# State loop and side-by-side experts: the skip term added on VectorE, expert pairs packed into one matmul output, and a new order of loads and gathers

## What is computed

```
# layer 0, state-space block, 8 heads of 64, per row tile
y   = Y_diag + Y_off            # (C B^T * decay mask) @ x  +  (C @ state) * exp(cumsum)
y   = y + x * D                 # the skip term
u   = u + (y * silu(z)) @ w_out     # times a gate from the adaLN vector
# layer 0, experts: 64 experts, top 8 of a softmax, at most 64 rows each
h2  = layer_norm(u) * scale + shift
sel = top_k(softmax(h2 @ gate_w.T), 8)
out[e] = (silu(rows[e] @ wg[e]) * (rows[e] @ wu[e])) @ wd[e]     # inner width 96
u   = u + gate * sum over the 8 of weight * out[expert, slot]
# layer 1: attention in a window of 64, 16 heads of 128; then an MLP of 2048 whose weights
# are 4-bit codes with scales: W = LUT[code] * scale
```

## Time and profile before

| | us |
|---|---|
| median of 3 runs | 800.57 |
| lowest and highest | 797.09, 804.24 |
| span of the profiled execution | 801.1 |

### The profile page before, as it was taken

The page is one execution under the profiler, slowest core; times in us unless marked ns, Lnnn a source line. Parts: engine busy times, 40 slices in busy tenths (PEclk is TensorE's granted clock), DMA queues, the critical chain, the costliest instruction groups (busy, mean ns, idle before and its releaser), DMA issues.

```text
span 801.1 us, 9617 instructions
## 1 busy us (share of the span) xinstructions
PE 620.3 (77%) x3248; PEld 469.8 (59%) x3248; DVE 508.0 (63%) x1121; ACT 283.7 (35%) x887; POOL 249.7 (31%) x288
## 2 busy tenths in 40 slices
PE   2997988740109789975385898898988789998996
PEld 0544766530008677763163665666666668887885
DVE  5547567833997536724677789889757636655444
ACT  2644544400103222332255665646646431111110
POOL 1228003275650000137545255251101126640000
PEclk9999999965559956987577999999999999999999
DMA  8900001049017996863112043150000000000000
GB/s 317 351 1 0 1 2 47 34 147 299 3 42 205 278 281 222 244 195 98 45 48 49 5 54 37 17 53 1 0 1 1 1 0 1 1 1 27 1 1 27
DMA packets 29808, 62.83 MB, mean 78 GB/s; under 512 B 5827, under 2 KB 13297, under 8 KB 29184
## 3 DMA queue, kind: packets, MB, share of 16 engines
q1 hardware_dynamic: 22336, 45.42, 18.1%
q0 software_dynamic: 7424, 16.80, 9.3%
HBM read 48.56 MB, written 17.83 MB: 83 GB/s over the span
## 4 chain that ended last, share of the span: by engine, by line
PE 53%; DVE 21%; issue 8%; ACT 8%; DMA 6%; POOL 2%; another core or an unknown queue 1%; SPq 1%; POOLq 0%; DVEq 0%; ACTq 0%
PE bank L1104 47%; DMA arena<-expert_in 4%; DVE arena L1054 2%; POOL expert_in L396 2%; ACT arena L594 2%; DVE arena L1013 2%; PE bank L1326 2%; PE bank L1444 1%; DVE arena L968 1%; DMA expert_out<-arena 1%; PE bank L1272 1%; ACT arena L612 1%; DMA arena<-in_wmod 1%; DVE arena L1002 1%
## 5 line engine op out<-in xcount | busy, mean ns | idle before, releaser
L1104 PE MATMUL bank<-arena 128*96 128x64 f32 (+9 forms) x2040 | 425.2, 367 | 64.0 <-issue 26.0
L1104 PEld LDWEIGHTS bank<-arena 128*128 128x128 f32 (+4 forms) x2040 | 295.3, 192 | 160.6 <-issue 100.9
L396 POOL DMA_INDIRECT expert_in<-arena x64 | 65.2, 1019 | 88.7 <-DVE arena L857 70.1
L410 POOL DMA_INDIRECT arena<-expert_out,arena x64 | 72.6, 1134 | 19.0 <-issue 18.5
L692 ACT ACTIVATE arena<-bank 128x512 f32<-128x512 f32 x32 | 19.1, 598 | 112.4 <-PE bank L1104 112.4
L1085 DVE TENSOR_TENSOR arena<-arena,bank 128x512 f32<-128x512 f32 x32 | 22.0, 687 | 56.1 <-ACT arena L692 56.1
L594 ACT ACTIVATE arena<-bank,arena 128x128 f32<-128x128 f32 x128 | 45.2, 383 | 25.2 <-DVE arena L1006 25.2
L1104 PE MATMUL bank<-h_hi,gu_hi 128*128 128x512 f32 x128 | 50.8, 397 | 0.5 <-ACT arena L695 0.5
L1104 PE MATMUL bank<-h_low,gu_hi 128*128 128x512 f32 x128 | 50.5, 394 | 0.0
L1104 PE MATMUL bank<-h_hi,low 128*128 128x512 f32 x128 | 50.1, 391 | 0.0
L434 POOL TENSOR_TENSOR low<-arena,gu_hi 128x128 fp32r<-128x128 f32 x64 | 29.7, 495 | 60.4 <-DVE dn_hi L1017 60.4
(11 more groups left out here) (200 smaller groups left out, 1024.2 us busy)
## 6 DMA issues: line engine op xcount, KB each, us to landing
arena<-in_wgu SPq DMA_DIRECT2D x32, 384.0 KB, 6.5
arena<-in_wd SPq DMA_DIRECT2D x32, 192.0 KB, 8.9
expert_in<-arena SPq DMA_DIRECT2D x1, 4096.0 KB, 23.9
arena<-expert_in SPq DMA_DIRECT2D x16, 256.0 KB, 7.2
expert_out<-arena POOLq DMA_DIRECT2D x16, 256.0 KB, 6.5
arena<-in_w SPq DMA_DIRECT2D x1, 2048.0 KB, 9.3
arena<-in_wmod SPq DMA_DIRECT2D x1, 1536.0 KB, 15.0
arena<-in_w_in SPq DMA_DIRECT2D x1, 1288.0 KB, 8.8
```

Source lines behind the costliest of these rows:

```text
L396: pool.indirect_dma_start(xin, bass.IndirectOffsetOnAxis(scatter8[:, t, k:k + 1], 0), h[:, t, :], None, bounds_check=SLOTS - 1, oob_is_err ...
L410: pool.indirect_dma_start(gath[t % 2][:, k, :], None, yex, bass.IndirectOffsetOnAxis(gather8[:, t, k:k + 1], 0), bounds_check=SLOTS - 1, o ...
L1104: return pe.matmul(o, lhsT, rhs, start=start, stop=stop, **kw)
```

## The change

Five things change in one diff.

1. **State loop.** It has two iterations fewer (`T + 2`). The skip term `xD[s]` is added on DVE to `yo_s`, and the sum to bank 3; the identity product goes. `w_out` is multiplied once by the gate (POOL), so the residual is one addition. The norm only subtracts and divides; scale and shift of h2 are applied by ACT as it copies transposed rows (`h2_cols`), both for the logits and in the experts. Softmax sums are left to one pass after the loop. Tiles are chosen and placed one by one, at s = t + 2. PE's order is new: transposes of h2 first, diagonal products late.
2. **Loads.** Nothing of the expert weights is loaded in the front; 12 pairs go out one after the other during the loop, one pair and one chunk of codes after it. Rows of `expert_in` are loaded on POOL's queue.
3. **Experts.** The rows are now stationary and the weights move (192 columns), two experts side by side in the two halves of the output's partitions. The product of gate and up is transposed (`hidden_T`, two a group) and copied by ACT. Results are copied out in one instruction, with three buffers.
4. **Decoding** takes 4 instructions instead of 7 for each half chunk.
5. **Gathers.** Tiles 0 and 1 ahead of the attention loop, then tile t + 2 after the rotary product of tile t.

Semaphores are merged and renamed too (`rowsT_mm`, `rowsT_ready`, `var_ready` and others). The diff, cut to its core:

```diff
-            for q in range(4):
+            for q, tile, early in ((0, 1, True), (1, 2, True), (2, 2, True), (3, 3, True), (6, 3, True), (12, 4, True), (4, 1, False),
+                                   (5, 2, False), (7, 4, False), (8, 5, False), (9, 6, False), (10, 7, False)):
+                sp.wait_ge(st_mm if early else yT_mm, tile)
                 load_pair(q)
             sp.wait_ge(yT_mm, T)
-            load_codes(0)
-            load_codes(1)
-            for q in range(4, NS):
-                load_pair(q)
-            for n in range(2, NEARLY):
+            load_pair(11)
+            for n in range(NEARLY):
                 load_codes(n)
...
+            def load_rows(g):
+                if g >= NX:
+                    pool.wait_ge(xgT_mm, g - NX + 1)
+                pool.dma_start(xg[g % NX], xin[4 * CAP * g:4 * CAP * (g + 1), :].rearrange("(q p) c -> p q c", p=P))\
+                    .then_inc(xg_loaded[g % NX], 16)
...
             for g in range(NG):
-                pool.wait_ge(ob_ready, 2 * (g + 1))
-                pool.dma_start(yex[4 * CAP * g:4 * CAP * (g + 1), :].rearrange("(e s) c -> s e c", s=CAP), ob[g % 2])
+                if g + NX < NG:
+                    load_rows(g + NX)
+                pool.wait_ge(ob_ready, g + 1)
+                pool.dma_start(yex[4 * CAP * g:4 * CAP * (g + 1), :].rearrange("(q p) c -> p q c", p=P), ob[g % 3])
...
-            for t in range(3):
-                gather(t)
+            gather(0)
+            gather(1)
...
-                if t + 3 < T:
-                    gather(t + 3)
+                if t + 2 < T:
+                    gather(t + 2)
...
--            for s in range(T + 4):
+            for s in range(T + 2):
+                if 0 <= s - 2:
+                    less_maximum(s - 2)
                 if s < T - 1:
                     state_after(s)
+                if 0 <= s - 2:
+                    choose(s - 2)
                 if s + 1 < T:
                     make_M(s + 1)
                 if 0 <= s - 1 < T:
...
-                    link(dve.tensor_tensor(h[:, t, :], bank[7][:, 0:DM], mod[0][:, 2, :], ALU.mult))
-                    dve.tensor_tensor(x[:, t, :], x[:, t, :], h[:, t, :], ALU.add).then_inc(x1_ready, 1)
+                    dve.tensor_tensor(x[:, t, :], x[:, t, :], bank[7][:, 0:DM], ALU.add).then_inc(x1_ready, 1)
...
+                if s < T:
+                    skip, y = xD[s], un_y[:, s % 2, :]
+                    if s >= 1:
+                        dve.wait_ge(yo_ready, s)
+                        link(dve.tensor_tensor(skip, skip, yo_s, ALU.add))
+                    dve.wait_ge(Yd_mm, s + 1)
+                    link(dve.tensor_tensor(y, skip, bank[3][:, :], ALU.add))
+                    dve.tensor_tensor(zs[:, s, :], zs[:, s, :], y, ALU.mult).then_inc(y_ready, 1)
...
-                    link(normed(h[:, t, :], x[:, t, :], t, mv[2], rstd[2]))
-                    link(dve.tensor_tensor(h[:, t, :], h[:, t, :], mod[0][:, 4, :], ALU.mult))
-                    dve.tensor_tensor(h[:, t, :], h[:, t, :], mod[0][:, 3, :], ALU.add).then_inc(h2_ready, 1)
+                    normed(h[:, t, :], x[:, t, :], t, mv[2], rstd[2]).then_inc(h2_ready, 1)
+                if 0 <= s - 2:
+                    place_rows(s - 2)
...
-                    mm(bank[3][:, :], ident, xD[s], start=True, stop=False, skip_group_check=True)
...
             def gate_up(g):
...
-                for e in range(4):
-                    for a in range(2):
-                        for j in range(KC):
-                            ins = mm(bank[2 + g % 2][0:FI, (4 * a + e) * CAP:(4 * a + e + 1) * CAP], w[:, a, j, :],
-                                     xgT[g % 2][:, 2 * (e // 2) + j, (e % 2) * CAP:(e % 2 + 1) * CAP], start=j == 0, stop=j == KC - 1)
+                for i in range(2):
+                    for j in range(KC):
+                        for e in range(2):
+                            ins = mm(bank[2 + g % 2][64 * e:64 * e + CAP, 2 * FI * i:2 * FI * (i + 1)],
+                                     xgT[g % 2][:, 2 * i + j, 64 * e:64 * e + CAP], w[:, :, j, :], start=j == 0, stop=j == KC - 1)
+            def hidden_T(g):
+                for i in range(2):
+                    ins = pe.transpose(bank[4 + g % 2][0:FI, i * P:(i + 1) * P], hid[g % 2][:, i, :], ident)
```

More of the change, by code:

```diff
@@ L90, in adaln_two_layers @@
         scatter8 = at(small + 432, T, TOPK).bitcast(u32)
+        h2_cols = at(small + 498, 2 * KC)
         wbc = at(small + 496, 1)
@@ L152, in adaln_two_layers @@
         PAIR = 4 * KC * FI + 2 * DM
-        slot_at = [X0 + PAIR * i if i < 4 else A0 + PAIR * (i - 4) for i in range(NS)]
+        slot_at = [X0 + PAIR * (i + 1) if i < 3 else A0 + PAIR * (i - 3) if i < 6 else X0 if i == 6 else A0 + PAIR * (i - 4) for i in range(NS)]
         wgu_s = [at(o, 2, 2 * KC * FI) for o in slot_at]
@@ L393, in _ @@
             for t in range(T):
-                pool.wait_ge(slots_ready, 1 + sum(t > last for last in LAST))
+                pool.wait_ge(slots_ready, t + 1)
                 for k in range(TOPK):
@@ L1298, in down @@
+            def down(g):
+                pe.wait_ge(hidT_ready, g + 1)
+                if g >= 2:
+                    pe.wait_ge(ob_ready, g - 1)
+                for i in range(2):
+                    for e in range(2):
+                        ins = mm(bank[6 + g % 2][64 * e:64 * e + CAP, i * DM:(i + 1) * DM],
+                                 hidT[g % 2][:, i * P + 64 * e:i * P + 64 * e + CAP], wd_s[(2 * g + i) % NS][:, e, :])
                 ins.then_inc(down_mm, 1)
-            pe.wait_ge(slots_ready, len(BATCHES))
+            pe.wait_ge(place_read, T)
@@ L1304, in _ @@
                     rows_T(g + 1)
+                if g >= 1:
+                    hidden_T(g - 1)
                 gate_up(g)
```

420 lines of the change are left out of this document (193 added, 227 removed).

## The result

The changed kernel takes 831.0 us (median of 4 executions, 829.67 to 832.97); the kernel before, timed beside it, 802.4. The medians differ by 29 us. The ratio is 1.038, 95% interval [1.032, 1.044]: slower. (It leaves out the slow one of the four executions of the kernel before, 811.64.) The prediction was 790, faster by 1%. Its direction was wrong, and 831 lies outside its range.

The account below looks back on a forecast made before the run. Bounds: POOL's scatters end the state loop, which PE paces; DMA and PE alternate in the experts; DVE is attention's busiest chain. 801.1 - 33.5 - 8 - 4 + 35 = 790.6, median 0.5 below: 790 us, range 774 to 812.

Parts of the forecast that it names:

- Both gaps of POOL: State loop: POOL idle 13.0 and 8.1 us between scatters, the second blamed on loads; closing only these gives -21 us.
- the burst: Loads from 172 to 200 us, nine pairs and two chunks, 6.4 MB at 275 GB/s; predicted to be gone.
- the loop's start, which does not move: State loop: its start stays, so tile 0 has slots at about 108 us instead of 130.
- The round, 12.1 to 12.2 us: State loop: a chain of 8.0 us on PE and 4.1 on DVE makes 12.1 us, 0.7 longer than before.
- slots late: Rival, state loop: PE's 2 us wait for h2 lowers its clock, six rounds 1.5 us longer; 797 us, chance 0.13.
- The headline edit: State loop: identity product leaves PE (0.87 us a round), DVE gets one addition (0.69 us); by itself no gain.
- the diagonal products lie beside it: State loop: the diagonal products are off the round's chain of 12.1 us across PE and DVE.
- the chain of 4.1 us on DVE: State loop: residual, moments, skip, y, product with z and norm, with handovers, before PE can transpose the next h2.
- hide under PE's 5.1: Experts: decoding on DVE and the product, at most 4.5 us a group, hide under PE's 5.1 us.
- The limit of 270 GB/s: Experts: DMA is the bound, 23.8 MB at 270 GB/s take 88 us up to the start of the last group.
- it has those 6.5 us to spare: Attention: PE idles 8 us more each time and returns at half clock, but has 6.5 us spare at the end.
- The bound of +45 for attention: Attention: upper bound of the +35 us cost, with the half clock on the chain.

Follow-up runs that it names:

- the run with PE kept busy: The changed kernel with six unread products of 256 columns added at the end of each state-loop iteration, filling PE's wait for h2: ratio to before 1.032.
- the kernel before with the late gathers: The kernel before with one edit: gathers of two tiles ahead of the attention loop, then those of tile t + 2, as in the changed kernel: ratio 1.076.
- The edits of the codes' order: Two separate edits of the changed kernel: two chunks decoded ahead, ratio to before 1.038; codes from the third chunk on issued on POOL's queue, ratio 1.029.
- the kernel with the lost rows spread: The changed kernel, with zero-weight assignments that found no room reading scattered rows of expert_out instead of all reading its last row: ratio to before 1.030.
- with the gathers ahead: The changed kernel with only the gather order put back: three tiles ahead of the attention loop, then those of tile t + 3: ratio to before 0.969.

## Why the prediction was wrong, step by step

**State loop and scatter, -33.5 predicted, -23.5 measured.** Both gaps of POOL and the burst ended, as predicted; the cause given for the second gap, the full DMA, is not borne out. Tile 4's first scatter was put at 108 + 4 x 12.2 = 156.8 and came at 167.4. Two terms make up the 10.6:
- Slots of tile 0 at 108; they came at 112.8 and the scatter at 113.9, 5.9 later. The step that failed is "the loop's start, which does not move": it moved by 4.0. POOL's new product was put at nothing because POOL had time; the DVE instruction beside it took 2.38 us, and PE behind that waited and had the half clock for longer. The other 1.9 are the working of the first iterations and the start of the scatter.
- The round, 12.1 to 12.2 us, was 13.44: 1.2 each over four rounds. This is the rival "slots late". The prediction gave it 0.13 because no row showed a gap of 2 us in the loop; the run with PE kept busy shows its size, 1.7 us on PE's part of the round (9.8 for 8.1), of which DVE's part, 3.6 for 4.1, gave 0.5 back.

From there POOL needed 43.7 us for four tiles, against 43.3. The second gap of POOL was priced at 8 us of the gain; the kernel before with the late gathers has no such gap, and its first gather comes no earlier for it (356.2 against 355.4).

**The headline edit "by itself gives nothing": wrong.** The step that failed is "the diagonal products lie beside it". They lie behind the output product, and so did the identity product. It is worth 0.7 us a round in the new order and 0.6 to 0.9 in the old one. The addition on DVE costs nothing, since it fills a wait. The 0.69 us for it stood in the chain of 4.1 us on DVE, which measured 3.6.

**Experts, -12 predicted, -7.2 measured.** PE's group was put at 5.1 us. Timeline of PE, transposes of rows, transposes of hidden, then all 24 records of gate, up and down of a group:

```profile
306.94 0.66 PE L1258 MATMUL bank<-arena 128*128 128x128 f32 x4
307.63 0.42 PE L1280 MATMUL bank<-arena 128*96 128x128 f32 x2
307.98 2.38 PE L1097 MATMUL bank<-arena 128*64 128x192 f32 x24
```

That is 3.4 us, and 2.38 for what I had put at 2.6 + 1.7 = 4.3, at a clock of 1.00: two experts do run side by side. The rule of the Trainium skill, "TensorEngine Tiling (Array Packing)", section Tiling Modes, that tiles work in parallel, agrees with this row; the drain that it warns of at a change of mode leaves no gap in these rows (307.63 + 0.42 to 307.98). It made no difference to the time, as said, for DMA binds. What failed was the overlap: I let the decoding "hide under PE's 5.1" and did not ask when its codes land. They stand behind weights on one queue, DVE waits for them in order, and the hidden product behind DVE. The edits of the codes' order gave 4 to 6 us, about the miss of 5. The limit of 270 GB/s was too low as well: the prediction called 275 the highest rate of a stretch, but the kernel before moves 335 GB/s in its first 40 us, and the changed one 293 for 60 us here. Over the whole stage it is 258: the two lulls at the ends stay (the DMA engines are 0.77 busy from 220 to 240 and from 300 to 320).

**Attention, +35 predicted, +57.5 measured.** The mechanism, DVE waiting for rows that are gathered in the same iteration, was right, and so was its count. Its size was not. Measured from the first gather, the eight `maxima` come later than before by steps of 2.9, 7.1, 12.4, 11.1, 10.8, 10.9, 0.3 and 0.0 us, and the end by 2.0 more. Predicted were 6.2, 3.2, 7.6 and three times 6.5, and 1.5 less ahead of them. A full iteration was to cost 6.5 and cost 11.1. The terms:
- Landing, 1.9 us from the earlier trace rows, is 4.8 in these iterations: +2.9. I took the row of tile 0 for all tiles. The loop's own gathers before were waited for by nobody, so no wait could show it; the DMA share of their stretch would have (0.62 at 68 GB/s from 489 to 505 in the kernel before).
- The half clock, "it has those 6.5 us to spare": wrong. From the first `maxima` to the next L1047 it is 14.93 us against 13.71, +1.2, here and in the kernel with the lost rows spread (512.37 - 490.48 less 6.96), and 13.71 again with the gathers ahead, where PE does not stand for that long.
- The rest, 0.5, is the wait's own working.

Windows of this iteration in the changed kernel, up to the end of the wait and behind it; the clock is the figure behind ACT and POOL:

```profile
478.10:504.90 26.80, 21.06 (x114) 15.30 (x112) 14.76 (x26) 8.37 (x25) 10.85 (x9) 1.00 0.33 40
504.90:518.50 13.60, 6.79 (x15) 3.94 (x16) 11.86 (x23) 8.26 (x30) 2.39 (x1) 0.50 0.01 1
```

PE is at 1.2 GHz for the 13.6 us behind the wait, after 10.9 us without work (500.1 to 511.0); in the kernel before it is at 1.00 from 501 to 516. L1047 then waits 1.90 us instead of 0.63.

**The range.** The bound of +45 for attention had the half clock on the chain and nothing for the landing. All three stages missed together, which no rival had; the upper end, 812, is only 21 us above the forecast, less than attention's miss alone.

## What to carry to other kernels

When an edit turns a transfer that nobody waited for into one that somebody does, price it from that transfer's own rows (its DMA share too), for in its old place a slow one shows nowhere. When work moves between two engines, ask on each what stands directly behind it: here a product with spare time on its engine in sum was on the chain, and an addition on the busier engine filled a wait. Work given to an engine with time to spare is free only if nothing beside it slows down: look at what its neighbours do meanwhile. And a new wait of 2 us per round on TensorE is to be priced with the half clock behind it, not only with its length.

## What the runs showed of the hardware

- An indirect DMA whose descriptors mostly read one row keeps the DMA engines 0.63 busy at 77 GB/s; with the rows spread 0.26, and the last of eight lands 1.9 us behind its issue instead of 4.8.
- PE idle for 1.84 us in a round of 13.4 brought the clock to 1.2 GHz for part of each round (mean 0.88); with the wait filled it stayed at 2.4 GHz (1.00) and the round took 12.4. In attention PE stood for 10.9 us in an iteration, and the clock of the 13.6 us from 504.9 on was 1.2 GHz (0.50).
- Products of 64 columns in the two halves of the array: 24 records in 2.38 us at the full clock, where one behind the other they would be 4.3 by the earlier trace rows.
- A DVE instruction of 128x128 elements took 0.76 us beside POOL products of 0.72 us and 2.38 beside one of 2.34.
- DMA engines 0.93 busy at 271 GB/s left small DVE instructions without waits in one trace, where another had 1.2 us ahead of each at 0.89 and 275 GB/s: the full DMA was not enough to cause them.
